# Global attention and the line memory as one block on Trainium2: the memory's first two tiles inside the last attention slot

## The reference, cut to what matters

```
scores  = q @ k.T * 8**-0.5, masked above the diagonal            # (4, 16, 1024, 1024)
seq_out = softmax(scores) @ v

w1, w2 = x_prev @ w1w.T, x @ w2w.T        # 4 numbers per head each; x_prev is x one token back
write  = exterior(w1, w2)                 # 6 products p1[i]*p2[j] - p1[j]*p2[i], divided by their norm
read   = exterior(x @ r1w.T, x @ r2w.T)
Jw     = write @ J6
M[t]   = sum over s < t of decay**(t - s) * outer(Jw[s], Jw[s])   # a 6x6 state per head and token, up to a power of decay
rd_M   = read @ M
mem_score = (1 - alpha) * sum(rd_M * read) + alpha * sum(rd_M * rd_M)
gated  = mean over heads of sigmoid(mem_score * mem_scale) * sigmoid(x @ memg_w.T)
out    = (seq_out + gated * (x @ memv_w.T)) @ out_w.T
```

## Time and profile before

| | us |
|---|---|
| median of three runs | 2012.93 (2011.08 to 2013.21) |
| profiled execution: its own time, its span | 2016.5, 2014.7 |
| global attention: first exponential to last values | 780.2 to 1165.33 |
| last slot, from the scores of its unit 1 | 1144.98 to 1165.33 |
| between the two blocks | 1165.33 to 1170.83 |
| memory: bodies -2 and -1 | 1170.83 to 1191.08 |
| one body of the memory in its steady state | 12.8 |
| first matmul of the output pass | 1293.45 |

### The profile page before, as it was taken

One profiled execution on the slowest core, in us unless ns is written; L12 is line 12 of the kernel. 1 busy time (PEld: TensorE's weight loads), 2 busy tenths in 40 slices (PEclk: granted clock), 3 DMA queues, 4 the chain that ended last, 5 costly groups with the idle time before them and its releaser, 6 DMA issues. The chain is left out here.

```text
span 2014.7 us, 52935 instructions
## 1 busy us (share of the span) xinstructions
PE 1918.5 (95%) x18490; PEld 1137.3 (56%) x18490; DVE 1630.2 (81%) x5442; ACT 1497.7 (74%) x4127; POOL 911.5 (45%) x538
## 2 busy tenths in 40 slices
PE   7999999999999979999999979799999999999998
PEld 4777764677774333344433357436777635777743
DVE  7999964899984379999999549769999648999844
ACT  5999983799995353777777844359999937999962
POOL 2788750688870150000000046218788505878700
PEclk9999999999999976999999999899999999999999
DMA  6212220121220040111111000002222201222301
GB/s 184 47 42 48 47 54 5 41 47 42 48 68 6 0 154 28 41 43 43 43 43 42 10 3 2 1 6 54 45 45 48 59 6 34 48 44 45 69 11 42
DMA packets 76107, 85.09 MB, mean 42 GB/s; under 512 B 17139, under 2 KB 50499, under 8 KB 75715
## 3 DMA queue, kind: packets, MB, share of 16 engines
q1 hardware_dynamic: 75551, 81.67, 16.4%
q10 hardware_dynamic: 292, 0.03, 0.0%
HBM read 21.14 MB, written 8.39 MB: 15 GB/s over the span
## 5 line engine op out<-in xcount | busy, mean ns | idle before, releaser
L304 ACT ACTIVATE probs<-probs,negmax 128x128 f32<-128x128 f32 x1024 | 399.9, 396 | 24.0 <-DVE negmax L377 23.1
L1642 ACT ACTIVATE gprobs<-ps_global 128x1024 f32<-128x1024 f32 (+3 forms) x384 | 290.7, 811 | 121.0 <-PE ps_global L1508 100.4
L259 POOL TENSOR_TENSOR rot<-rot 128x1024 f32<-128x1024 f32 x128 | 302.3, 2362 | 141.3 <-DVE rot L347 141.3
L265 POOL TENSOR_TENSOR qk<-rot,cnorm 128x1024 f32<-128x1024 f32 x128 | 243.8, 1904 | 120.0 <-POOL rot L259 90.5
L272 POOL TENSOR_TENSOR probs<-probs,iden 128x1024 f32<-128x1024 f32 x128 | 242.8, 1897 | 120.3 <-DVE iden L385 120.3
L1572 DVE TENSOR_REDUCE maxes<-ps_global 128x1 f32<-128x512 f32 (+2 forms) x384 | 222.1, 638 | 11.2 <-PE ps_global L1471 6.7
L377 DVE CUSTOM_DVE_ANT_0 probs<-ps_attn,masks 128x128 f32<-128x128 f32 x1024 | 225.7, 284 | 0.3 <-issue 0.3
L1466 PE MATMUL ps_global<-ks,qs 48*128 48x512 bf16 (+3 forms) x768 | 198.3, 348 | 15.5 <-DMA ks<-split_scratch 9.5
L304 ACT ACTIVATION_READ_ACCUMULATOR probs<-probs,negmax 128x1 f32 x1024 | 197.1, 193 | 0.0
L345 DVE TENSOR_TENSOR rot<-ps_attn,rotary 128x512 f32<-128x512 f32 x256 | 174.8, 683 | 2.1 <-PE ps_attn L171 1.6
L239 PEld LDWEIGHTS ps_attn<-probsT,v_first 128*64 128x64 f32 x2048 | 118.2, 136 | 98.1 <-ACT probsT L325 94.3
(11 more groups left out here) (207 smaller groups left out, 4621.0 us busy)
## 6 DMA issues: line engine op xcount, KB each, us to landing
v_first<-v_second SPq DMA_DIRECT2D x256, 128.0 KB, 2.3
hs<-z_a SPq DMA_DIRECT2D x256, 32.0 KB, 1.9
ln<-z_b SPq DMA_DIRECT2D x56, 128.0 KB, 2.3
split_scratch<-parts SPq DMA_DIRECT2D x8, 384.0 KB, 3.3
split_scratch<-gprobs SPq DMA_DIRECT2D x8, 384.0 KB, 4.7
qs<-split_scratch SPq DMA_DIRECT2D x32, 96.0 KB
ks<-split_scratch SPq DMA_DIRECT2D x32, 96.0 KB
x_tok<-in_x_dram SPq DMA_DIRECT2D x4, 512.0 KB, 6.5
```

The lines of the kernel that those rows point to most:

```text
L259: nc.gpsimd.tensor_tensor(a, a, b, ALU.add).then_inc(C["rot_sum"], 1)
L265: nc.gpsimd.tensor_tensor(qk[:, k % 2, :].rearrange("p (h d) -> p h d", d=DH), rot_a[:, k % 2, :, :], cnorm[:, k % 2, :].unsqueeze(2).to_b ...
L304: last = nc.scalar.activation(probs[:, k % 2, slot, :], probs[:, k % 2, slot, :], ACT.Exp, scale=-1.0, bias=negmax[:, k % 2, slot:slot + 1 ...
L1642: nc.scalar.activation(probs[:, step % RING, 2 * p:2 * p + 2, 0:w], ps[:, S0 + 2 * p:S0 + 2 * p + 2, 0:w], ACT.Exp).then_inc(C["p2_exp"], 1)
```

## The change

`memory_pass` goes as a block of its own; its code moves into `global_attention_pass`. Four things change in it.

1. The 16 line items of tiles 0 and 1 are issued by PE in the last slot, two in each of its units 0 to 7, one behind the scores of each pair of heads. The 16 one-column matmuls of tile 0's tail stand behind the values of unit 9. What follows bodies -2 and -1 on the other engines goes with them. DVE does the copies of the left halves and the squares of these two tiles itself, since ACT has its exponentials; the four `inverse` pairs stand on ACT behind the exponentials of units 4, 5, 9 and 10. The first state DMAs stand on SP in front of the last output DMAs. The loop of bodies begins at 0 and follows the last slot directly.
2. The memory's buffers lie over those of attention: `left`, `line`, `square`, `ssq`, `inv`, `state` and `term` over the ring of queries and keys (now one buffer `kq`), `mul` and `unit` over `parts`, `outer` over `v_all`, the rest over `gprobs`. DVE and POOL first wait until the scores of slot 14 are done. The outer products of tile 1 lie over values that the last slot reads, and wait for its last values (`p2_av`).
3. The PSUM banks are those of attention: lines in the banks of the first sweep, memory in those of the scores. The tail of tile 0 uses a line bank for half of its groups, so it waits for the product of item 14, and item 16 waits for the first `advance`. The memset of the tail banks goes.
4. The memset of ones in the layer norm pass becomes three of a third of the size.

```diff
-def global_attention_pass(nc, C, K, A, later_keys, y, v_all, qs, ks, scratch, o_all, den_all):
+LINE = 6
...
+TAILS_AT = 9
+INVERSES_AT = (4, 5, 9, 10)
...
+def query_key(kq, which, buf):
+
+    return kq[:, buf, which, :].bitcast(BF16).rearrange("k (p t) -> k p t", p=2)
...
+def global_attention_pass(nc, C, K, A, later_keys, y, v_all, kq, probs, scratch, o_all, den_all):
...
+        N = LROWS
+        LINES, MEMORY, TURN, TAIL_BANKS = M0, S0, S0 + 3, (M0 + 2, O0)
+        LAST = S_TILES - 1
+        STATE_ROWS = B * PAIRS_6
+        shared = Arena(kq[:, :, :, :].rearrange("p k w t -> p (k w t)"))
+        term = shared.take(AH * STATE_ROWS)
+        shared.at = 2 * T + TILE * 2
+        left = shared.take(4 * 2 * N).rearrange("p (n c) -> p n c", n=4)
+        line = shared.take(2 * HB * LINE).rearrange("p (w h b c) -> p w h b c", w=2, h=AH, b=B)
+        square = shared.take(2 * HB * LINE).rearrange("p (w x c) -> p w x c", w=2, x=HB)
+        ssq = shared.take(2 * HB).rearrange("p (w x) -> p w x", w=2)
+        inv = shared.take(2 * HB).rearrange("p (w x) -> p w x", w=2)
+        state = shared.take(2 * GROUPS * STATE_ROWS).rearrange("p (k q n) -> p k q n", k=2, q=GROUPS)
+        first = Arena(early[:, :])
+        mul = first.take(2 * B * 2 * N).rearrange("p (w b n) -> p w b n", w=2, b=B)
+        unit = first.take(4 * HB * LINE).rearrange("p (w k x c) -> p w k x c", w=2, k=2, x=HB)
+        outer = v_all[:, :, :, :].rearrange("p t h d -> p (t h d)").rearrange("p (k h n) -> p k h n", k=2, h=AH)
+        behind = Arena(blocks)
+        line_scores = behind.take(TOK)[0:AH, :]
+        read, plain, blend = [behind.take(HB * LINE).rearrange("p (x c) -> p x c", x=HB) for _ in range(3)]
+        weight = behind.take(HB * LINE).rearrange("p (h b c) -> p h b c", h=AH, b=B)
+        score = behind.take(B * AH).rearrange("p (b h) -> p b h", b=B)
...
+        def tail_of(k, q):
+            bank = TAIL_BANKS[q // 2] if k or q < 2 else LINES
+            return ps[:, bank, (q % 2) * STATE_ROWS:(q % 2 + 1) * STATE_ROWS]
...
+            def line_items(k, w, b):
+                n = item(k, w, b)
+                c = b * PAD + 1 + k * TILE
+                out = ps[:, LINES + n % 2, 0:4 * N].rearrange("p (f c) -> p f c", c=N)
+                if n == 0:
+                    pe.wait_ge(C["p1_free"], C.after("p1_free", USES))
+                if n == 2 * ITEMS:
+                    wait(pe, "ml_state", 1)
+                wait(pe, "ml_mul", n - 1)
+                nc.tensor.matmul(out[:, 0:4:3, :], y[:, c - 1 + w:c - 1 + w + TILE], A["wlines"][:, 4 * w:4 * w + 2, :], start=True,
+                                 stop=True, skip_group_check=True)
+                nc.tensor.matmul(out[:, 1:3, :], y[:, c:c + TILE], A["wlines"][:, 4 * w + 2:4 * w + 4, :], start=True, stop=True,
+                                 skip_group_check=True).then_inc(C["ml_proj"], 1)
...
+            def tails(k):
+                wait(pe, "ml_outer", k + 1)
+                wait(pe, "ml_state", k)
+                if k == 0:
+                    wait(pe, "ml_mul", 2 * ITEMS - 1)
+                if k == 1:
+                    pe.wait_ge(C["o_copied"], C.after("o_copied", 2 * SLOTS))
...
+            def items(n, first):
+                if n == SLOTS - 1 and first < 2 * ITEMS:
+                    line_items(first // ITEMS, first % ITEMS // B, first % B)
+                    items(n, 2 * u)
...
+                    items(n, 2 * u + 1)
                     values(n, u)
                     for use in uses_after(n, u, 2):
                         produce(use)
+                    if n == SLOTS - 1 and u == TAILS_AT:
+                        tails(0)
+            for t in range(S_TILES + 2):
+                body(t)
...
+            def copy_left(n):
+                wait(dve, "ml_proj", n + 1)
+                nc.vector.tensor_copy(left[:, n % 4, :], ps[:, LINES + n % 2, 0:2 * N]).then_inc(C["ml_left"], 1)
...
+            def first_squares(k, w):
+                wait(dve, "ml_line", 2 * k + w + 1)
+                wait(dve, "ml_ssq", 2 * k + w - 1)
+                row = line[:, w, :, :, :].rearrange("p h b c -> p (h b c)")
+                nc.vector.tensor_tensor(square[:, w, :, :].rearrange("p x c -> p (x c)"), row, row, ALU.mult
+                                        ).then_inc(C["ml_square"], 1)
+                sum_squares(k, w)
...
+            dve.wait_ge(C["p2_scores"], C.after("p2_scores", 2 * U2 * (SLOTS - 1)))
+            first_items(0, 6)
+            first_squares(0, 0)
+            first_items(6, 8)
+            first_squares(0, 1)
+            first_items(8, 10)
+            clip(0, 0)
+            first_items(10, 12)
+            clip(0, 1)
+            first_items(12, 14)
+            first_squares(1, 0)
+            first_items(14, 16)
+            first_squares(1, 1)
+            advance(0)
+            clip(1, 0)
+            clip(1, 1)
+            for t in range(S_TILES + 2):
+                body(t)
...
+            def outer_products(k):
+                wait(gp, "ml_unit", 2 * k + 1)
+                wait(gp, "ml_m", USES_M * (k - 1))
+                wait(gp, "ml_tail", k - 1)
+                if k == 1:
+                    gp.wait_ge(C["p2_av"], C.after("p2_av", U2 * SLOTS))
...
+            gp.wait_ge(C["p2_scores"], C.after("p2_scores", 2 * U2 * (SLOTS - 1)))
+            nc.gpsimd.memset(state[:, :, :, :], 0.0).then_inc(C["ml_set"], 1)
...
+                    if n == SLOTS - 1 and u in INVERSES_AT:
+                        inverse(*divmod(INVERSES_AT.index(u), 2))
             copy_out(SLOTS - 1, 1)
+            for t in range(S_TILES + 2):
+                body(t)
...
+            def pass_state(k):
+                if k == 0:
+                    wait(sp, "ml_set", 1)
+                else:
+                    wait(sp, "ml_state", k)
+                wait(sp, "ml_outer", k + 1)
+                if k < LAST:
+                    wait(sp, "ml_tail", k + 1)
+                for j in range(GROUP):
+                    sp.dma_start(outer[TILE - 1:TILE, k % 2, j:AH:GROUP, :], state[32 * j:32 * j + 1, k % 2, :, :]
+                                 ).then_inc(C[f"ml_row{k % 2}"], 16)
...
+            pass_state(0)
             put_out(SLOTS - 1, 1)
+            for k in range(1, S_TILES):
+                pass_state(k)
...
-def memory_pass(nc, C, K, A, y, scores):
...
             den_all = attention.enter_context(nc.sbuf_tensor("den_all", [P, CHUNK], F32))
+            gprobs = attention.enter_context(nc.sbuf_tensor("gprobs", [P, RING, GROUP, CHUNK], F32))
             with ExitStack() as seq:
                 v_all = seq.enter_context(nc.sbuf_tensor("v_all", [P, TILES, AH, AD + 1], F32))
-                qs = seq.enter_context(nc.sbuf_tensor("qs", [P, RING, 2, T], BF16))
-                ks = seq.enter_context(nc.sbuf_tensor("ks", [P, RING, 2, T], BF16))
+                kq = seq.enter_context(nc.sbuf_tensor("kq", [P, RING, 2, T], F32))
                 scratch = split_scratch(nc)
-                layernorm_pass(nc, C, K, x, z_a, lambda gp: nc.gpsimd.memset(ks[:, :, :, :], 1.0))
-                global_attention_pass(nc, C, K, A, dram["later_keys"], z_a, v_all, qs, ks, scratch, z_b, den_all)
-            with nc.sbuf_tensor("scores", [AH, TOK], F32) as scores:
-                memory_pass(nc, C, K, A, z_a, scores)
-                attention_output_pass(nc, C, K, A, z_a, scores, z_b, den_all, x)
+
+                def ones(gp):
+                    for buf in range(RING):
+                        nc.gpsimd.memset(query_key(kq, 1, buf), 1.0)
+
+                layernorm_pass(nc, C, K, x, z_a, ones)
+                global_attention_pass(nc, C, K, A, dram["later_keys"], z_a, v_all, kq, gprobs, scratch, z_b, den_all)
+            scores = gprobs[:, :, :, :].rearrange("p k h t -> p (k h t)")[0:AH, 0:TOK]
+            attention_output_pass(nc, C, K, A, z_a, scores, z_b, den_all, x)
         with ExitStack() as second:
             local_attention_pass(nc, C, K, W, *attention_probs(second), z_a, z_b, x, None)
         output_pass(nc, C, K, x, out)
```

More of the change, by code:

```diff
@@ new lines, in memory @@
+            def memory(k, j):
+                use = USES_M * k + j
+                if j == 0:
+                    wait(pe, f"ml_row{k % 2}", 16 * GROUP * (k // 2 + 1))
+                wait(pe, "ml_term", use - 2)
+                first, end = HEADS_AT[j]
+                for h in range(first, end):
+                    mm = nc.tensor.matmul(ps[:, MEMORY + use % 3, (h - first) * B * PAIRS_6:(h - first + 1) * B * PAIRS_6],
+                                          A["decay"][:, h, 0:TILE], outer[:, k % 2, h, :], start=True, stop=True,
+                                          skip_group_check=True)
+                mm.then_inc(C["ml_m"], 1)
@@ new lines, in turn, with body, lines, memories @@
+            def turn(k):
+                wait(pe, "ml_score", k + 1)
+                wait(pe, "ml_out", k)
+                for b in range(B):
```

(65 more changed lines are left out.)

481 lines of the change are left out of this document (173 added, 308 removed).

## The result

The changed kernel takes 1999.33 us as the median of four runs (1998.27 to 2000.08), against 2013.07 for four runs of before (2011.08 to 2016.95). The ratio is 0.9929, with a 95% interval of 0.9912 to 0.9946. Forecast were 1996.8 in a range of 1992 to 2002. Run again later it took 2001.63 against 2015.74, a ratio of 0.9927 (0.9914 to 0.9941). The profiled execution takes 2000.08 with a span of 1998.3, 16.4 less than before.

The account below looks back on a forecast made before the run. ACT sets the pace in the last slot, then a drain and latency chain, then DVE; PE becomes the slot's bound. 29.94 - 10.8 - 2.4 - 0.6 = 16.1 us off 2012.93 gives 1996.8, range 1992.0 to 2002.0.

Parts of the forecast that it names:

- What goes: From the end of the last values to body 0's first term: drain and bodies -2 and -1 vanish, 29.94 us.
- What the last slot grows by: Last attention slot: PE becomes the bound with the items added, so the slot of 20.35 us grows by 10.8.
- The chain: Last slot, line work through DVE, POOL and ACT from item 11 to the last inverse and values, ending at 31.7 us.
- the two counts: Last slot's length: first by PE's units 0 to 7 plus units 8 to 11, 30.3 us; second by the line chain, 31.7.
- The two prices that no row of before had: Last slot on DVE: copy of a left half at 0.34 us (0.2 to 0.5), square of 128x384 at 0.56.
- What costs nothing: Table load, memsets, laid-over buffers beyond the waits named, and SP's DMA order add no time.
- Body 0: First memory body after the slot: DVE following PE costs about 1.1 us, POOL's earlier start returns about 0.5; net 0.6.
- The rule on VectorE and GpSimd: DVE's four squares and POOL shut each other out of SBUF; 2.7 us on the chain if each met POOL, median 1999.5.
- A: Rival, last slot: items at 0.65 us, inverses never late, slot grows by 6.8; gain 20.1, 1992.8 us; chance 0.23.
- B: Rival, last slot: the chain holds up the exponentials, slot grows by 16; gain 11, 2002 us; chance 0.17.
- C: Rival, last slot: TensorE falls to 1.2 GHz, slot grows by 35.7, 2021.7 us; chance 0.06 with other ways to slower.
- D: Rival, last slot: items wait for a bank or buffer until slot 15 is nearly over; no change, 2013 us; chance 0.04.

Follow-up runs that it names:

- e5_items_before_square: Changed kernel with items 14 and 15 copied and multiplied on VectorE before the square of tile 1's write lines; slot 32.08 us, 0.71 shorter; execution 2003.73 us.
- e8_fill_and_late: Changed kernel with paired items, items 14 and 15 before the square, items 16 and 17 before the last values, last inverse late; 1995.61 us, ratio 0.9901.
- e3_items_paired: Changed kernel with a unit's two items together behind both pairs' scores; slot 1.45 us shorter (31.34), first term at 35.21 us against 35.14.

## Why the prediction was right, point by point

- **What goes, 29.94 us**: right, and it is made of 7.30 us for the single block, whose aftermath in the clock (1.80) the prediction named without a price, and the rest by overlap.
- **What the last slot grows by**: 12.44 instead of 10.8. This is the term that was mis-sized; with 0.2 more in body 0 and 0.05 less up to the first term it makes the 1.8 us between the 16.1 of the forecast and the 14.35. The mechanism was right. Units 0 to 7 took 24.98 us instead of 22.8, on two terms: an item costs 0.85 and not 0.76, as it pays the surcharge on both sides and the row that I took pays it on one; scores in front of an item take 0.30 on average, from 0.24 to 0.36 by their width (0.32 for 1152.43 to 1152.75), and not 0.25. 16 x 0.09 and 16 x 0.05 make 2.2, and that is what PE's stretch ran behind the forecast. Item 11, from which the line chain starts, left PE at 17.5 instead of 15.8, 1.7 late. The chain's later steps were only 1.0 to 1.2 late, and that is luck: the clip in it took 0.19 and not the 0.85 that I had put in.
- **The chain**: right step by step. POOL's outer products ended at 23.4 (forecast 22.3), the first sum at 25.5 (24.4), the product of item 15 at 26.8 (25.8), the last sum at 29.1 (27.9), the slot at 32.8 (31.7). Taking a middle between the two counts, 30.3 and 31.7, cost 0.5 of the 1.6 us; the other 1.1 is the chain's lateness. The first count, with the 24.98 put in, would give 32.5, so the two lie close together and `e5_items_before_square` took out 0.71 before the rest held. The queue behind the square was named beforehand; `e5_items_before_square` showed its price, 0.71.
- **The two prices that no row of before had**: DVE's copy takes 0.36 (forecast 0.34, range 0.2 to 0.5) and its square 0.55 or 0.56 (taken: 0.56). Both held.
- **What costs nothing**: right; item 16 and the first memory matmul waited for nothing.
- **Body 0**: 0.80 instead of 0.6. Its blend took 1.41 us beside a subtraction on POOL, where another body pays 0.61, and its weight 0.56 instead of 1.24; the rest is DVE following PE. Its parts weren't taken apart by an experiment.
- **The rule on VectorE and GpSimd** that the prediction names from the Trainium skill ("SBUF — State Buffer", the two separate sides of SBUF) did not bite at the squares of the changed kernel, since POOL was idle at all four (0.55 or 0.56 each), so the 2.7 us were not paid. The traces agree with the rule where the two engines met: a square that began beside a running subtraction took 1.35 (`e8_fill_and_late`), a subtraction that began beside a running square 1.25 instead of 1.00 (`e5_items_before_square`).
- **The rivals**: A failed on the item's price. B's mechanism, exponentials held up by an inverse, is there with 0.59 us and not with 5. C didn't occur in the slot, whose clock was 1.00; in `e3_items_paired` the clock did fall, after a wait at the slot's end and not among the items. D failed: the first item followed the slot's start by 0.36 us.

The measured median's gain, 13.7, and the stretch's, 14.35, agree; the 16.4 of the spans holds 1.74 of the start's scatter.

## What to carry to other kernels

When a pass is laid into another's holes, price its instructions where they alternate with the host's, not from a run of their own kind: here half an item cost 0.42 against 0.33, and an engine that was entered as busy 83% (16.82 of 20.35 us) took 2.8 of 13.6 us of items into its holes. Put nothing in front of a pacing instruction that waits on another engine's late result, and on an in-order engine put ready work ahead of waiting work. Making the bound engine faster can lengthen its last wait (2.19 us saved, 0.62 of it waited away again); look at what ends that wait too, or fill it.

## What the runs showed of the hardware that was not expected

- TensorE's granted clock after a wait does not follow from the wait's length alone. It was 0.60 over 3.87 us after one of 2.35 (`e3_items_paired`), which ate the shorter slot's whole gain, and 1.00 after one of 2.65 (the kernel before, at 1183.72); after the same wait of 1.82 us it was 0.64 in one execution of the changed kernel and 1.00 in another.
- The start of the same stretch scatters by 6.3 us over ten profiles of kernels that are alike up to there but for memsets and buffer places, while the stretch itself repeats within 0.02 us in the two pairs of like profiles. An edit worth less than that is read from the stretch.
